# Both units of twelve double groups multiplied in rounded parts, with GpSimd taking the new differences

## Chip, cores and metric

The kernel runs on one core of a Trainium2 chip (trn2). The metric is the time of the program on the device in microseconds, the median of three runs. The core has a matrix engine (PE, with its weight loads shown apart as PEld), VectorE (DVE), ScalarE (ACT), GpSimd (POOL) and SyncE (SP), which here issues nearly all DMAs.

## What is computed

The program is a small vision tower on four images of 512 tokens. Its first step, the embedding, is the part that is changed:

```python
def _L0_tok_ref(xyz, freq_bands, W):          # xyz: [4, 3, 512, 192]
    b, c, n, d = xyz.shape
    xb = 2.0 * jnp.pi * xyz[..., None] * freq_bands          # 6 bands
    feat = jnp.concatenate([jnp.sin(xb), jnp.cos(xb)], axis=-1)
    feat = feat.reshape(b, n, -1)                            # 6912 features
    return jnp.einsum('bnf,of->bno', feat, W)                # W: [192, 6912]

def reference(x, cls_tok, ...):
    h = _L0_tok_ref(x, L0_tok_freq_bands, L0_tok_W)
    h = jnp.concatenate([cls_tok per image, h], axis=1)
    h = h + attention block with relative positions(layernorm(h))
    h = h + second attention and a mixture of 8 experts(layernorm(h))
    return h
```

(Cut; the last lines tell the blocks in words.) For each token the 576 coordinates are multiplied by six frequencies, sine and cosine are taken of each product, and the 6912 features are multiplied by a 192 x 6912 matrix. Everything is float32.

## The kernel before

`program` calls `embed_phase` first, then attention, the second attention and the experts. All phases before and after the embedding are the same in both kernels.

**Groups.** The 576 coordinates of an image lie in five blocks of 128 partitions, for 512 tokens each (tile `x`). A unit is one block and one frequency, 512 columns wide. `GROUPS` lists fifteen groups: twelve double groups with two units (two blocks with one frequency, 1024 columns) and three single ones (the fifth block, 512 columns). `pairs` are the double groups. The four images are passed one after another; for image 0 the weights are loaded and prepared beside the work, the other images find them in SBUF.

**One group.** VectorE computes the product with the frequency, rounded to an integer (`whole`, tile `near`, line 202), subtracts it from the product, which leaves a turn between -0.5 and 0.5 (`reduce`, tile `turn`, line 210), and takes its absolute value (`absolute`, line 216, in the place of `near`). ScalarE takes the sine of the turn (line 347) and the cosine by the sine of the absolute value (line 349), into `feat`. All these tiles are rings of `NF = 3` groups.

**Two kinds of product.** Unit 0 of each group, and single groups, are multiplied natively (`native`, line 417): the float32 features are the stationary operand of PE, the float32 weights `w` with 192 columns the moving one; each float32 product stands in the trace as two records. Four blocks of 128 tokens with sine and cosine make eight products, sixteen records. Unit 1 of each double group is multiplied in rounded parts (`split`, lines 433 to 437): ScalarE casts the features to the rounded type F32R (`first_parts`, line 360), VectorE subtracts that from the features and so has the low part (`rest`, line 227); the weights are taken apart in the same way once, in image 0 (`split_weights`, lines 354 and 221). PE then multiplies high features by high and low weights in one product of 384 columns, and low features by high weights in one of 192, in PSUM banks `sums`, whose columns 0 to 191 and 192 to 383 are added afterwards.

**Order on the engines.** Each engine runs its program in the order of the code. VectorE's `image` does, for group g: `reduce(g)`, `whole(g + 2)`, `absolute(g)`, `rest(g - 1)`; in image 0 `split_weights(g)` follows; in later images `take_sums` of the image before follows in group 1, and `normalize` in group 4. `whole` waits until the cosine three groups back is done, `reduce` until the sine is. ScalarE does sine, cosine and the cast, in image 0 the weights between them, after group 3 the square roots of the image before and after group 10 the transposed tokens. ScalarE's sine waits on `feat_free`, PE's end of the group three back. PE does `native(0)`, `native(1)`, `split`. GpSimd's only work for each image is one addition (line 184, `base`, 128x768) when the sums are taken; SP stores the result with a DMA. `stand_alone` adds one to a semaphore that nobody waits for.

The last image's last three groups are multiplied by `last_groups` in another order, so that the sums end bank by bank.

Of the kernel before, what the change touches and what calls it, by code (L numbers as in the profile page):

```python
# [18 lines left out]
B = 4  # L19
# [50 lines left out]
def embed_phase(nc, s):  # L70
# [9 lines left out]
    w_hi, w_lo, hi_done, lo_done = sem("w_hi"), sem("w_lo"), sem("hi_done"), sem("feat_lo")  # L80
    pairs = [g for g in range(NE) if GROUPS[g][1] == 2]
    NPAIR = len(pairs)
    sums_done, tokens_done, stated, aggregated = sem("sums_done"), sem("tokens_done"), sem("stated"), sem("aggregated")
# [8 lines left out]
    with ExitStack() as ctx:  # L92
        sb = lambda n, sh, dt=F32: ctx.enter_context(nc.sbuf_tensor(n, sh, dt))
        x = sb("x", [128, 5, N])
# [30 lines left out]
        def _(sp):  # L125
            sp.sem_inc(kept, 16)
            sp.dma_start(freq[:, :], s.d["freq_cols"]).then_inc(freq_in, 16)
            for g in range(NE):
# [4 lines left out]
                sp.dma_start(w[:, 2 * g:2 * g + 2, :], s.d["tok_wT"][k0:k0 + 2].rearrange("k p n -> p k n")).then_inc(w_in[g], 16)  # L133
# [38 lines left out]
        def _(pool):  # L172
# [168 lines left out]
        def _(act):  # L341
# [36 lines left out]
            for g in range(NE):  # L378
# [5 lines left out]
                group(0, g, True)  # L384
                if g in pairs:
# [15 lines left out]
        def _(pe):  # L401
            pe.sem_inc(h1_flipped, 2)

            def group(b, g, first):
                n, r = GROUPS[g][1], g % NF
                if first:
                    pe.wait_ge(w_in[g], 16)

                def native(j):
                    pe.wait_ge((sin_done, cos_done)[j], b * NE + g + 1)  # L410
                    k = 2 * g + j
                    for m in range(4):
                        ends = g == NE - 1 and j == 1
                        begins = g == j == 0
                        if begins and not first:
                            pe.wait_ge(tokens_done, b * 4 - 3 + m)
                        mm = pe.matmul(sums[m][:, 0:D], feat[:, r, j, 0, 128 * m:128 * m + 128], w[:, k, :],  # L417
                                       start=begins, stop=ends)
# [4 lines left out]
                def split():  # L423
# [4 lines left out]
                    for j in range(2):  # L428
                        for m in range(4):
                            f = lambda part: parts[:, r, part, j, 128 * m:128 * m + 128]  # L430
                            if g == j == 0:
                                for part in range(2):
                                    pe.matmul(sums[m][:, part * D:part * D + D], f(0), w_parts[:, g, j, part, :], start=False, stop=False)
                            else:
                                pe.matmul(sums[m][:, 0:2 * D], f(0), w_parts[:, g, j, :, :].rearrange("p a n -> p (a n)"),  # L435
                                          start=False, stop=False)
# [2040 lines left out]
```

## Time and profile before

| | us |
|---|---|
| median of three runs (lowest, highest) | 993.34 (992.94, 995.34) |
| the profiled execution, its time | 992.54 |
| its span in the trace | 990.8 |
| PE busy | 896.9 (91%) |
| VectorE busy | 696.6 (70%) |
| ScalarE busy | 645.6 (65%) |
| GpSimd busy | 142.0 (14%) |
| the embedding, from the span's start to the last image's sums | about 290 |

The busy shares are means over stages that differ, so they tell little of one stage; the views by stretch and the timelines do. Times in a timeline row are the start and the duration of one instruction; durations of neighbours on one engine overlap a little, so the distance from start to start tells better what an instruction costs a queue without pauses. Matmul durations overlap by much.

### The profile page before, as it was taken

The numbers are of one execution on the slowest core, as the hardware profiler recorded it, in microseconds if no ns is written. First come the engines' busy times: TensorE is split into PE (matmuls) and PEld (weight loads), VectorE is DVE, ScalarE is ACT, GpSimd is POOL, SyncE is SP. The second block draws the span as 40 slices with busy tenths as digits, with TensorE's granted clock in tenths as the row PEclk, the third lists the DMA queues.
The fourth block names the chain that finished last, engine by engine and source line by source line (L and its number), as shares of the span: only waits on it lengthen the run. The fifth ranks groups of instructions, "written<-read, shape, count | busy, mean of one in ns | idle before, by whom it ended". The sixth has DMA issues, their size and how long they took to land. (4 is left out here: it accounts for less than half of the span.)

```text
span 990.8 us, 19970 instructions
## 1 busy us (share of the span) xinstructions
PE 896.9 (91%) x6459; PEld 794.4 (80%) x6459; DVE 696.6 (70%) x1643; ACT 645.6 (65%) x1218; POOL 142.0 (14%) x204
## 2 busy tenths in 40 slices
PE   6999999999988899989998999898699996699996
PEld 5999999999976677667767776676498875699995
DVE  6889859769633796488648864887556335687775
ACT  5767757649624797589758974987444331886862
POOL 1000000000000144114311441244300000000000
PEclk9999999999997899999999999999789997799997
DMA  8021101089812696169526952795300020443201
GB/s 275 23 71 51 44 27 37 21 125 149 128 34 70 185 293 174 51 210 298 160 58 205 297 156 62 216 294 138 107 1 1 18 87 24 119 164 97 72 2 64
DMA packets 83801, 114.11 MB, mean 115 GB/s; under 512 B 12271, under 2 KB 44476, under 8 KB 83724
## 3 DMA queue, kind: packets, MB, share of 16 engines
q1 hardware_dynamic: 82636, 112.39, 41.2%
q8 instruction: 37, 0.61, 0.3%
q10 hardware_dynamic: 1088, 0.79, 0.2%
q14 instruction: 40, 0.33, 0.1%
HBM read 62.31 MB, written 47.67 MB: 111 GB/s over the span
## 5 line engine op out<-in xcount | busy, mean ns | idle before, releaser
L417 PE MATMUL psum<-w,feat 128*128 128x192 f32 x912 | 160.4, 331 | 11.9 <-ACT feat L347 9.0
L417 PEld LDWEIGHTS psum<-w,feat 128*128 128x128 f32 x912 | 149.3, 192 | 12.8 <-issue 10.3
L646 POOL TENSOR_SCALAR a_scores<-a_scores,a_inv 112x514 f32<-112x514 f32 (+1 forms) x160 | 113.0, 707 | 268.1 <-DVE a_inv L1018 267.9
L1003 DVE CUSTOM_DVE_ANT_0 a_scores<-psum,a_bias 112x514 f32<-112x514 f32 (+1 forms) x160 | 110.0, 688 | 46.6 <-PE psum L722 38.2
L875 ACT ACTIVATE a_scores<-a_scores,a_least 112x514 f32<-112x514 f32 (+1 forms) x160 | 116.7, 729 | 9.8 <-DVE a_least L1003 9.1
L735 PE MATMUL psum<-ident,a_scores 112*112 112x112 f32 (+1 forms) x800 | 100.2, 256 | 18.1 <-DVE a_probsT L1013 10.8
L435 PE MATMUL psum<-w_parts,parts 128*128 128x384 f32 x368 | 113.7, 374 | 0.8 <-DVE parts L227 0.8
L347 ACT ACTIVATE feat<-turn 128x1024 f32<-128x1024 f32 (+1 forms) x60 | 58.4, 974 | 82.5 <-PE psum L437 43.4
L735 PEld LDWEIGHTS psum<-ident,a_scores 112*112 112x112 f32 (+1 forms) x800 | 75.3, 134 | 40.3 <-issue 19.4
L722 PE MATMUL psum<-a_kh,a_q 128*112 128x258 f32 (+1 forms) x320 | 99.6, 333 | 1.0 <-DVE a_least L1003 1.0
L437 PE MATMUL psum<-w_parts,parts 128*128 128x192 f32 x384 | 96.6, 252 | 0.0
L673 PE MATMUL psum<-h1T,place 96*128 (+3 forms) x320 | 87.2, 407 | 4.7 <-DVE a_q L967 2.2
L870 ACT COPY a_probsT<-psum 112x336 f32<-112x336 f32 (+1 forms) x160 | 66.5, 416 | 28.5 <-PE psum L735 24.2
L722 PE MATMUL psum<-a_kl,a_q 128*112 128x258 f32 (+1 forms) x320 | 83.9, 283 | 0.0
L704 PE MATMUL psum<-a_table,a_qpos 96*112 96x257 bf16 (+1 forms) x320 | 66.3, 289 | 10.0 <-ACT a_pos L862 5.4
L862 ACT COPY a_pos<-psum 112x514 f32<-112x514 f32 (+1 forms) x92 | 54.1, 588 | 31.2 <-PE psum L704 28.7
L437 PEld LDWEIGHTS psum<-w_parts,parts 128*128 128x128 f32 x384 | 73.3, 191 | 0.0
L673 PEld LDWEIGHTS psum<-h1T,place 96*128 96x128 f32 (+1 forms) x320 | 59.5, 201 | 15.6 <-DVE a_q L967 2.9
L210 DVE SCALAR_TENSOR_TENSOR turn<-x,freq,near 128x1024 f32<-128x1024 f32 (+1 forms) x60 | 70.9, 1182 | 0.3 <-DVE h1T L331 0.3
L435 PEld LDWEIGHTS psum<-w_parts,parts 128*128 128x128 f32 x368 | 69.2, 188 | 1.3 <-issue 1.3
L202 DVE TENSOR_SCALAR near<-x,freq 128x1024 int32<-128x1024 f32 (+1 forms) x60 | 41.6, 695 | 40.3 <-ACT feat L349 32.5
L349 ACT ACTIVATE feat<-near,half_pi 128x1024 f32<-128x1024 f32 (+1 forms) x60 | 63.3, 1055 | 4.8 <-DVE near L216 4.7
(297 smaller groups left out, 1808.2 us busy)
## 6 DMA issues: line engine op xcount, KB each, us to landing
shear<-a_pos SPq DMA_DIRECT2D x128, 224.9 KB, 3.7
a_bias<-shear SPq DMA_DIRECT2D x128, 224.4 KB, 3.7
shear<-zero SPq DMA_DIRECT2D x20, 448.9 KB, 15.7
e_fc<-in_e_fc_dram SPq DMA_DIRECT2D x16, 384.0 KB, 3.9
x<-in_xT_dram SPq DMA_DIRECT2D x20, 256.0 KB, 3.0
e_proj<-in_e_proj_dram SPq DMA_DIRECT2D x8, 576.0 KB, 5.4
shear<-a_pos SPq DMA_DIRECT2D x32, 130.5 KB
a_bias<-shear SPq DMA_DIRECT2D x32, 130.3 KB
```

Source lines behind the costliest of these rows:

```text
L210: dve.scalar_tensor_tensor(out=turn[:, r, 0:n, :], in0=x[:, c0:c0 + n, :], scalar=freq[:, u:u + 1], in1=near[:, r, 0:n, :], op0=ALU.mult, ...
L417: mm = pe.matmul(sums[m][:, 0:D], feat[:, r, j, 0, 128 * m:128 * m + 128], w[:, k, :], start=begins, stop=ends)
L435: pe.matmul(sums[m][:, 0:2 * D], f(0), w_parts[:, g, j, :, :].rearrange("p a n -> p (a n)"), start=False, stop=False)
L437: mm = pe.matmul(sums[m][:, 0:D], f(1), w_parts[:, g, j, 0, :], start=False, stop=False)
L646: pool.tensor_scalar(row, row, inv[0:TILES[g % NT][1], g % TT:g % TT + 1], 1.0, ALU.mult, ALU.mult).then_inc(weighed, 1)
L673: mm = pe.matmul(out[:, 0:HALF], wt[0:rows, c, 128 * p:128 * p + 128], x, start=c == 0, stop=c == 1)
L704: mm = pe.matmul(pairs[2][w][0:r, 0:HALF], qpos[:, h, i0:i0 + r], table[:, w * HALF:w * HALF + HALF], start=True, stop=True)
L722: mm = pe.matmul(pairs[score_pair(g)][w][0:r, 0:HALF + 1], q[:, h, i0:i0 + r], k[:, h, w * HALF:w * HALF + HALF + 1], start=k is kh, stop= ...
L735: mm = pe.transpose(pairs[3][jb // 3][0:TILE, TILE * (jb % 3):TILE * (jb % 3) + r], scores[0:r, g % TT, TILE * jb:TILE * jb + TILE], s.ide ...
L870: act.copy(probsT[:, slot(g // NT), 0:3, i0:i0 + r], src).then_inc(put_a, 1)
L875: act.activation(scores[0:r, g % TT, 0:PADL], scores[0:r, g % TT, 0:PADL], ACT.Exp, bias=least[0:r, g % TT:g % TT + 1], scale=-1.0, accum_ ...
L1003: dve.tensor_tensor_reduce(halves(scores[0:r, g % TT, 0:PADL]), psum2(score_pair(g), r), halves(bias[0:r, g % MR, :]), -1.0 / 8, BIG, ALU. ...
```

## The change

Unit 0 of every double group now goes the way of unit 1.

- Weights: tile `w` shrinks to the three single groups (`w_native`). The weights of unit 0 of the double groups land in the tile `w_first`, at the place of their low parts; ScalarE casts them into the high parts (`split_first_weights` on ScalarE), GpSimd subtracts in place (`split_first_weights` on GpSimd). This happens in image 0.
- Features: ScalarE casts unit 0 (`high[..., 0, :]`, counted by `first_hi`) and then unit 1, as before. GpSimd subtracts the cast of unit 0 from the features in place (`first_rest`, counted by `first_lo`), VectorE that of unit 1, now in place too. `over` lays a float32 tile and a rounded one over the same memory.
- PE: a double group is `split(1)`, then `split(0)`; each waits for its weights (image 0), its cast and its difference. The first product of an image now is one of 384 columns that starts the accumulation, and it waits for the sums of the image before, bank by bank. Single groups stay as they are.
- GpSimd: the addition for an image comes after `first_rest` of group 3 of the next image.
- The program is built with a smaller scratch for dynamic DMAs (1024).

```diff
         x = sb("x", [128, 5, N])
-        w = sb("w", [128, 2 * NE, D])
+        w_native = sb("w_native", [128, len(native_units), 2, D])
+        w_place, w_first = over("w_first", [128, NFULL, 2, 2, D])
+        first_raw = lambda g: w_place[:, before(g), :, 1, :]
         raw = s.place.rearrange("p (g j n) -> p g j n", g=NPAIR, j=2)
-        feat = sb("feat", [128, NF, 2, 2, N])
+        feat, feat_place = over("feat", [128, NF, 2, 2, N])
         w_parts = sb("w_parts", [128, NPAIR, 2, 2, D], F32R)
-        parts = sb("parts", [128, NF, 2, 2, N], F32R)
+        high = sb("high", [128, NF, 2, 2, N], F32R)
...
-            pool.wait_ge(rows_in, 16)
-            for b in range(B):
+
+            def split_first_weights(g):
+                pool.wait_ge(first_w_hi, before(g) + 1)
+                pool.tensor_tensor(w_first[:, before(g), :, 1, :], first_raw(g), w_first[:, before(g), :, 0, :].bitcast(F32),
+                                   ALU.subtract).then_inc(first_w_lo, 1)
+
+            def first_rest(b, g):
+                r = g % NF
+                pool.wait_ge(first_hi, b * NFULL + before(g) + 1)
+                stand_alone(pool, passed)
+                pool.tensor_tensor(feat_place[:, r, :, 0, :], feat[:, r, :, 0, :], high[:, r, :, 0, :].bitcast(F32), ALU.subtract).then_inc(first_lo, 1)
+
+            def make_base(b):
                 pool.wait_ge(tokens_done, b * 4 + 4)
                 pool.wait_ge(kept, b * 16 + 16)
+                pool.wait_ge(rows_in, 16)
                 pool.tensor_tensor(base[:, :, :], tokens[:, :, :], b2_rows[:, :].unsqueeze(1).broadcast_to([128, 4, D]), ALU.add).then_inc(base_set, 1)
+
+            for g in full:
+                split_first_weights(g)
+                first_rest(0, g)
+            with pool.Fori(1, B) as b:
+                for g in full:
+                    first_rest(b, g)
+                    if g == 3:
+                        make_base(b - 1)
+            make_base(B - 1)
...
-                dve.tensor_tensor(parts[:, r, 1], feat[:, r, :, 1, :], parts[:, r, 0].bitcast(F32), ALU.subtract).then_inc(lo_done, 1)
+                dve.tensor_tensor(feat_place[:, r, :, 1, :], feat[:, r, :, 1, :], high[:, r, :, 1, :].bitcast(F32), ALU.subtract).then_inc(lo_done, 1)
...
+            def split_first_weights(g):
+                act.wait_ge(w_in[g], 16)
+                act.copy(w_first[:, before(g), :, 0, :], first_raw(g)).then_inc(first_w_hi, 1)
+
             def first_parts(b, g):
                 r = g % NF
                 act.wait_ge(sin_done, b * NE + g + 1)
                 act.wait_ge(cos_done, b * NE + g + 1)
-                act.copy(parts[:, r, 0], feat[:, r, :, 1, :]).then_inc(hi_done, 1)
+                if g in full:
+                    act.copy(high[:, r, :, 0, :], feat[:, r, :, 0, :]).then_inc(first_hi, 1)
+                act.copy(high[:, r, :, 1, :], feat[:, r, :, 1, :]).then_inc(hi_done, 1)
...
                 group(0, g, True)
+                if g in full:
+                    split_first_weights(g)
                 if g in pairs:
                     split_weights(g)
                     first_parts(0, g)
...
+                def split(unit):
+                    weights = w_parts[:, g] if unit else w_first[:, before(g)]
                     if first:
-                        pe.wait_ge(w_lo, g + 1)
-                    pe.wait_ge(hi_done, b * NPAIR + g + 1)
-                    pe.wait_ge(lo_done, b * NPAIR + g + 1)
+                        pe.wait_ge(*((w_lo, g + 1) if unit else (first_w_lo, before(g) + 1)))
+                    if unit:
+                        pe.wait_ge(hi_done, b * NPAIR + g + 1)
+                        pe.wait_ge(lo_done, b * NPAIR + g + 1)
+                    else:
+                        pe.wait_ge(first_hi, b * NFULL + before(g) + 1)
+                        pe.wait_ge(first_lo, b * NFULL + before(g) + 1)
                     for j in range(2):
...
+                            if g == j == 0 and unit == 1:
+                                if not first:
+                                    pe.wait_ge(tokens_done, b * 4 - 3 + m)
+                                pe.matmul(sums[m][:, 0:2 * D], hi, both, start=True, stop=False)
                             else:
...
-                mm = native(0)
-                mm = native(1)
-                if n == 2:
-                    mm = split()
+                if g in full:
+                    split(1)
+                    mm = split(0)
+                else:
+                    native(0)
+                    mm = native(1)
...
-    nc = bacc.Bacc("TRN2", target_bir_lowering=False, num_devices=1)
+    nc = bacc.Bacc("TRN2", target_bir_lowering=False, num_devices=1, dynamic_dma_scratch_size=1024)
```

## Rows read from the trace of the kernel before

**Rows 1.** Page, part 1: engine, busy us, share of the span, instructions.

```profile
PE 896.9 (91%) x6459; PEld 794.4 (80%) x6459; DVE 696.6 (70%) x1643; ACT 645.6 (65%) x1218; POOL 142.0 (14%) x204
```

**Rows 2.** Table by stretches: busy us of each engine (instructions), PE clock, DMA.

```profile
160.00:180.00 20.00, 20.00 (x132) 20.00 (x132) 19.75 (x29) 16.96 (x18) 0.00 (x0) 1.00 0.14 46
280.00:300.00 20.00, 16.74 (x99) 15.28 (x100) 10.06 (x29) 4.30 (x8) 2.27 (x6) 0.84 0.05 21
```

**Rows 3.** Timeline of PE, one double group: start, duration, engine, line, tiles, count.

```profile
126.71 2.79 PE L417 MATMUL psum<-w,feat 128*128 128x192 f32 x16
...
129.20 0.47 PE L435 MATMUL psum<-w_parts,parts 128*128 128x384 f32 x1
...
131.59 2.79 PE L417 MATMUL psum<-w,feat 128*128 128x192 f32 x16
```

**Rows 4.** Timeline of VectorE in image 2, one turn of its loop.

```profile
156.32 1.27 DVE L210 SCALAR_TENSOR_TENSOR turn<-x,freq,near 128x1024 f32<-128x1024 f32 x1
157.52 0.74 DVE L202 TENSOR_SCALAR near<-x,freq 128x1024 int32<-128x1024 f32 x1
158.18 0.68 DVE L216 TENSOR_SCALAR near<-turn 128x1024 uint32<-128x1024 uint32 x1
158.78 1.21 DVE L227 TENSOR_TENSOR parts<-feat,parts 128x1024 fp32r<-128x1024 f32 x1
159.92 1.27 DVE L210 SCALAR_TENSOR_TENSOR turn<-x,freq,near 128x1024 f32<-128x1024 f32 x1
```

**Rows 5.** Timeline of ScalarE in image 2, from one sine to the next.

```profile
164.29 1.06 ACT L347 ACTIVATE feat<-turn 128x1024 f32<-128x1024 f32 x1
...
167.59 1.06 ACT L347 ACTIVATE feat<-turn 128x1024 f32<-128x1024 f32 x1
```

**Rows 6.** Timeline of image 0's first group, and the weight split by source line.

```profile
8.97 5.23 PE L417 MATMUL psum<-w,feat 128*128 128x192 f32 x16 [8.97 <-ACT feat L347]
...
9.03 1.15 ACT L349 ACTIVATE feat<-near,half_pi 128x1024 f32<-128x1024 f32 x1 [0.21 <-DVE near L216]
...
10.09 0.49 ACT L354 CAST w_parts<-place 128x384 fp32r<-128x384 f32 x1
...
10.49 1.04 ACT L360 CAST parts<-feat 128x1024 fp32r<-128x1024 f32 x1
...
L221 DVE TENSOR_TENSOR w_parts<-place,w_parts x12: 557/559/559, 10.6 to 64.2; 128x384 fp32r<-128x384 f32 x12
```

**Rows 7.** GpSimd's two-input operations by line: count, ns min/median/max, first and last start.

```profile
L184 POOL TENSOR_TENSOR base<-tokens,b_rows x4: 1803/1810/1813, 82.5 to 289.7; 128x768 f32<-128x768 f32 x4
...
L638 POOL TENSOR_TENSOR a_parts<-a_rest,a_parts x8: 1095/1130/1177, 301.3 to 594.5; 128x514 bf16<-128x514 f32 x8
```

**Rows 8.** Timeline of GpSimd and VectorE where image 1's sums are taken.

```profile
151.10 1.81 POOL L184 TENSOR_TENSOR base<-tokens,b_rows 128x768 f32<-128x768 f32 x1 [66.75 <-DVE tokens L236]
...
152.51 1.48 DVE L210 SCALAR_TENSOR_TENSOR turn<-x,freq,near 128x1024 f32<-128x1024 f32 x1
```

**Rows 9.** A tensor_scalar by source line, and GpSimd's timeline beside its first start.

```profile
L1648 DVE TENSOR_SCALAR t_yn<-y,t_inv x16: 298/308/1878, 706.6 to 737.7; 128x192 f32<-128x192 f32 x16
...
704.69 3.66 POOL L1228 MEMSET t_x<- 1x2048 f32 x2
```

**Rows 10.** Timeline in the attention: a VectorE copy, two GpSimd operations alike.

```profile
580.92 0.67 DVE L939 COPY a_h<-h1T 97x1028 f32 x1
...
579.37 0.70 POOL L646 TENSOR_SCALAR a_scores<-a_scores,a_inv 112x514 f32<-112x514 f32 x1 [0.98 <-DVE a_inv L1018]
...
581.20 0.96 POOL L646 TENSOR_SCALAR a_scores<-a_scores,a_inv 112x514 f32<-112x514 f32 x1 [1.13 <-DVE a_inv L1018]
```

**Rows 11.** Timeline of VectorE after image 1's sums, and line 233 by source line.

```profile
148.83 1.14 DVE L233 COPY tokens<-psum 128x192 f32<-128x192 f32 x4
...
165.12 1.25 DVE L285 TENSOR_SCALAR h_tok<-tokens,mean_var,inv 128x192 f32<-128x192 f32 x4
...
L233 DVE COPY tokens<-psum x12: 343/346/350, 80.2 to 218.5; 128x192 f32<-128x192 f32 x12
```

More of the change, by code:

```diff
@@ L80, in embed_phase @@
     w_hi, w_lo, hi_done, lo_done = sem("w_hi"), sem("w_lo"), sem("hi_done"), sem("feat_lo")
+    first_w_hi, first_w_lo, first_hi, first_lo = sem("first_w_hi"), sem("first_w_lo"), sem("first_hi"), sem("first_lo")
     pairs = [g for g in range(NE) if GROUPS[g][1] == 2]
     NPAIR = len(pairs)
+    full = pairs
+    NFULL = len(full)
+    before = lambda g: sum(e < g for e in full)
+    native_units = [g for g in range(NE) if g not in full]
     sums_done, tokens_done, stated, aggregated = sem("sums_done"), sem("tokens_done"), sem("stated"), sem("aggregated")
@@ L93, in embed_phase, with over @@
         sb = lambda n, sh, dt=F32: ctx.enter_context(nc.sbuf_tensor(n, sh, dt))
+        def over(n, sh):
+            with nc.sbuf_tensor(n, sh, F32) as plain:
+                pass
+            return plain, sb(f"{n}_parts", sh, F32R)
         x = sb("x", [128, 5, N])
-        w = sb("w", [128, 2 * NE, D])
+        w_native = sb("w_native", [128, len(native_units), 2, D])
+        w_place, w_first = over("w_first", [128, NFULL, 2, 2, D])
+        first_raw = lambda g: w_place[:, before(g), :, 1, :]
         raw = s.place.rearrange("p (g j n) -> p g j n", g=NPAIR, j=2)
-        feat = sb("feat", [128, NF, 2, 2, N])
+        feat, feat_place = over("feat", [128, NF, 2, 2, N])
         w_parts = sb("w_parts", [128, NPAIR, 2, 2, D], F32R)
-        parts = sb("parts", [128, NF, 2, 2, N], F32R)
+        high = sb("high", [128, NF, 2, 2, N], F32R)
         near = sb("near", [128, NF, 2, N], I32)
@@ L132, in _ @@
                 k0 = 2 * first_unit[g]
-                sp.dma_start(w[:, 2 * g:2 * g + 2, :], s.d["tok_wT"][k0:k0 + 2].rearrange("k p n -> p k n")).then_inc(w_in[g], 16)
+                first = first_raw(g) if g in full else w_native[:, native_units.index(g)]
+                sp.dma_start(first, s.d["tok_wT"][k0:k0 + 2].rearrange("k p n -> p k n")).then_inc(w_in[g], 16)
                 if g in pairs:
@@ L405, in group @@
                 n, r = GROUPS[g][1], g % NF
-                if first:
+                if first and g not in full:
                     pe.wait_ge(w_in[g], 16)
@@ L410, in native @@
                     pe.wait_ge((sin_done, cos_done)[j], b * NE + g + 1)
-                    k = 2 * g + j
+                    k = native_units.index(g)
                     for m in range(4):
                         ends = g == NE - 1 and j == 1
[L414 to L418, printed above, removed]
+                        mm = pe.matmul(sums[m][:, 0:D], feat[:, r, j, 0, 128 * m:128 * m + 128], w_native[:, k, j, :],
+                                       start=False, stop=ends)
                         if ends:
@@ L428, in split @@
                     for j in range(2):
+                        both = weights[:, j, :, :].rearrange("p a n -> p (a n)")
                         for m in range(4):
[L430 to L433, printed above, removed]
-                            else:
-                                pe.matmul(sums[m][:, 0:2 * D], f(0), w_parts[:, g, j, :, :].rearrange("p a n -> p (a n)"),
-                                          start=False, stop=False)
@@ L437, in split @@
-                            mm = pe.matmul(sums[m][:, 0:D], f(1), w_parts[:, g, j, 0, :], start=False, stop=False)
-                    return mm
-                mm = native(0)
-                mm = native(1)
-                if n == 2:
-                    mm = split()
+                            hi = high[:, r, j, unit, 128 * m:128 * m + 128]
+                            lo = feat_place[:, r, j, unit, 128 * m:128 * m + 128]
+                            if g == j == 0 and unit == 1:
+                                if not first:
+                                    pe.wait_ge(tokens_done, b * 4 - 3 + m)
+                                pe.matmul(sums[m][:, 0:2 * D], hi, both, start=True, stop=False)
+                            else:
+                                pe.matmul(sums[m][:, 0:2 * D], hi, both, start=False, stop=False)
@@ L444, in group @@
+                            mm = pe.matmul(sums[m][:, 0:D], lo, weights[:, j, 0, :], start=False, stop=False)
+                    return mm
+                if g in full:
[4 more added lines that the diff above has]
+                    mm = native(1)
                 if g < NE - 1:
@@ L467, in last_groups @@
                         for j in range(2):
-                            mm = pe.matmul(sums[m][:, 0:D], feat[:, g % NF, j, 0, 128 * m:128 * m + 128], w[:, 2 * g + j, :],
+                            mm = pe.matmul(sums[m][:, 0:D], feat[:, g % NF, j, 0, 128 * m:128 * m + 128], w_native[:, native_units.index(g), j, :],
                                            start=False, stop=g == NE - 1 and j == 1)
```

1 line of the change is left out of this document (removed).

## The prediction

> **What bounds the kernel now.** I read the page's busy table first: the matrix engine (PE) is busy 91% of the span, no other engine over 70% [rows 1]. That mean covers several stages, so I went to the table by stretches. The edit lies in the embedding alone, about the first 290 us, and there PE is busy 20.00 of 20.00 us at full clock, while the stretches behind it, where PE has pauses, come at a lower granted clock [rows 2]. So PE bounds the embedding, and what a double group costs PE is the next view: its timeline shows native matmuls at 126.71, the split ones from 129.20, and the next native ones at 131.59 [rows 3]. A double group is 4.88 us of PE, 2.49 for the native unit and 2.39 for the split one. The other engines follow: VectorE's timeline in a stretch without pauses gives turn 1.20, near 0.66, absolute 0.60, rest 1.14 (start to start), together 3.60 us a group [rows 4]; ScalarE takes 3.30 [rows 5]. Both have over a microsecond of room beside PE's 4.88, and GpSimd is nearly empty. The reader is to see that only PE is full, and then to ask whether the room on the others is really free.
>
> **PE's part.** Unit 0 of each of the 48 double groups (12 in each of 4 images) leaves the native form and takes the form unit 1 has. A split unit runs inside a group at 2.39 less its first, slower pair: 129.20 to 131.59 has eight pairs with about 0.10 of change-over, so 2.29. The group becomes 2 x 2.29 = 4.58 instead of 4.88, a gain of 0.30 us, 48 times, 14 us, if PE stays the bound. The three single groups stay native, 2.49 each.
>
> **ScalarE's part.** One more cast per double group, by the row of the cast that is there (about 1.0 start to start): 3.30 becomes 4.3, still under 4.58. In image 0 one more weight copy of 0.49, started 0.40 before the next instruction [rows 6].
>
> **GpSimd's part, and its price.** The subtraction of 128x1024 is new there. The nearest row is its addition of 128x768 f32 with two inputs from SBUF: 1.81 us; the other two-input form, 128x514 with bf16 output, takes 1.13 [rows 7]. By size these give 2.41 and 2.25. I take 2.35, from the first row, with 0.19 of it as a fixed part (next paragraph). In image 0 come twelve weight subtractions of 128x384, 0.81 + 0.19 = 1.00 by the same row. Rounded output in place is shown by no GpSimd row; VectorE's same step writes rounded output at the plain price, so I add nothing, and allow 2.25 to 2.8. The Trainium skill (GPSIMD Engine Reference, section 3.1) gives 4497 ns for a two-input addition of 2048 columns; half of it is 2.25, an estimate by that page, with which the sum would be about 5 us lower.
>
> **Is VectorE's room free while GpSimd works?** This decides, and the trace has places where both are at work on SBUF. The turn operation, which has two SBUF inputs, takes 1.27 alone [rows 4]; where it starts 0.40 before the end of a GpSimd addition it takes 1.48 [rows 8], longer by 0.20. A tensor_scalar of 0.31 (the median of its line) takes 1.88 when it starts in the middle of a GpSimd memset that ends at 708.35: it was through at 708.47 [rows 9]. So it did not run slower: it stood still until 0.19 before GpSimd's recorded end, and then took its usual time; the turn operation gives the same 0.20. The other way round, GpSimd's 0.70 operation, started in the middle of a VectorE copy between SBUF tiles, took 0.96 [rows 10]. Both wait, and each for the whole of the other's instruction. All four operations of VectorE's embedding loop are of the kinds in these rows: turn and rest have two SBUF inputs, near and absolute are tensor_scalars that read 1024 columns in 0.60 to 0.75, faster than the two-input ones, as the held copy does. So I cost GpSimd's subtraction not beside VectorE's work but in line with it, at 2.35 - 0.19 = 2.16 us.
>
> The Trainium skill (SBUF — State Buffer, section Who interferes with whom) has this as an exclusive lock on a port pair, held for the whole instruction. The rows agree except for the last 0.19 us. By the rule alone the sum would be 48 x 0.19 = 9 us higher; I go by the rows.
>
> **Images 1 to 3.** What must pass one after another is now: twelve groups of 3.60 + 2.16 = 5.76, 69.1 us; three single groups, whose three operations I take at 1.5 (between half and all of the 2.46 of a double group), 4.5; taking the sums, 148.83 to 152.51, 3.7 [rows 8, 11]; normalising, two runs of four at 1.25, 2.5 [rows 11]; GpSimd's own addition, 1.81 - 0.19 = 1.6. One subtraction lies beside the taking of the sums, whose operations read PSUM or one SBUF tile: less 2.2. That is 79.2 us an image against PE's 12 x 4.58 + 3 x 2.49 = 62.4, so VectorE and GpSimd together are the new bound. Before, the additions that follow each image's sums start at 82.5 and, three images on, at 289.7 [rows 7]: 69.1 an image. Longer by 10.1 each, three times 30.
>
> **Image 0.** Here ScalarE's and GpSimd's weight steps stand in the chain too. Count from the end of absolute(g), by the prices above: VectorE does rest(g-1) to 1.1 and then waits for the weight copies; ScalarE does the cosine and two copies, the first ready at 1.6, the second at 2.0; GpSimd splits the first weights from 1.6 and lets go at 2.4; VectorE splits its own (0.5, by its row of 0.56 [rows 6]) to 3.0, then turn(g+1) to 4.2; GpSimd, ready since the cast ended at 2.9, subtracts until 6.3; near(g+3) and absolute(g+1) end at 7.6. So 7.6 us a group. Absolute(0) ends at 9.0, since the cosine starts at 9.03 on its release [rows 6]; absolute(11) then at 92.6. From there the cosine, the copies, the first cast and the subtraction end at 97.8 or so, rest(11) at 99, PE's last double group at 103.6 and three single ones at 111.2. Before, the sums of image 0 are taken from 80.2 on [rows 11]. Longer by 31.
>
> **The sum.** 30 + 31 = 61 us. The profiled execution took 992.5 (span 990.8 and 1.7 around it), the median of the runs is 993.3, 0.8 more. 993.3 + 61 = 1054 us, slower by 6%. What follows the embedding is the same instructions and moves as a block. The kept rows of an image are now added after group 3 of the next; they leave by a DMA that has a whole image of time, so that costs nothing but the 1.6 counted. SP's queue gets no new wait, the weights come in the same number of transfers, and every DMA of the embedding is issued by SP, so the smaller scratch is costed at nothing.
>
> **Clock.** PE would now be busy some 80% in images 1 to 3 and 60% in image 0. In the row of before with 16.74 busy of 20 us the granted clock is 0.84, some of it at the lower level of 1.2 GHz [rows 2]; at that level sixteen native records took 5.23 at the start instead of 2.49 [rows 3, 6]. A double group would then take some 9.2 (twice 4.58), 1.6 over the 7.6 of its turn in image 0. Bounds: nothing, and 12 x 1.6 = 19 us if all of image 0 meets it; images 1 to 3 keep PE fuller. I put nothing into the sum and the 19 into the range.
>
> **Rivals.**
> *The wait is one-sided* (VectorE, once it runs, does not hold GpSimd back, so half an operation, some 0.45 us, is saved at each of 48 subtractions and the weight steps): 1054 - 22 = 1032 us. Against it: 0.96 in place of 0.70 [rows 10].
> *No waiting at all on these operations.* Then PE gains 14; image 0 gives back some 6, since ScalarE's 5.2 a group and the later start of the first product bind there; and each later image gives back about 2: PE used to do the native unit of groups 0 and 1 while VectorE took the sums (3.7) and caught up (3.6 to rest(1)), and now nothing of group 1 can start before rest(1) ends, 7.3 after the sums, while group 0 is through at 1.5 + 4.6 = 6.1; ScalarE's roots cost another microsecond at group 4. 14 - 6 - 6 leaves about 2: 991 us, no difference. For it: the added work fits each engine alone.
> *PE's gain comes through* (the other side): as before, but with the three features in the ring covering those pauses, 14 - 6 = 8 us: 985 us, faster. It decides at the point where VectorE's 3.60 and what GpSimd holds back stay under 4.58, that is if a subtraction costs VectorE less than 1.0 us in place of 2.16. The stretched rows speak against it [rows 8, 9].
>
> **How the numbers follow.** Full waiting both ways 0.80 (1040 to 1085, by three terms: subtraction at 2.25 to 2.8 is 48 x -0.1 to +0.45, -5 to +22; the clock, to +19; and the chain of image 0, in which small waits can fall out, to -10); one-sided 0.08; none 0.05; gain 0.07. The range 1028 to 1085 leaves out the last two and the tails of the first. A measurement here tells about 0.3%, 3 us, from no change: faster 0.07, same 0.05, slower 0.88.
>
> **What would show it.** In the trace of the changed kernel: GpSimd subtractions of 2.2 to 2.8; turn, near, absolute or rest stretched by up to 2.2 in every double group, the sum of VectorE's starts near 5.8 a group; PE idle before its split matmuls, released by VectorE or GpSimd; the additions after the sums some 80 us apart instead of 69; image 0's sums taken near 111. If VectorE's operations keep their lengths, the step on waiting is wrong; if PE's native-free group isn't near 4.6 where nothing waits, the first step is.

## The result, and the profile after

The changed kernel takes 1063.7 us (median of 4 runs, 1057.4 to 1067.4) against 993.1 for the kernel before in the same runs (4 runs, 986.5 to 995.3): a ratio of 1.072, interval 1.067 to 1.077. It is slower by 71 us; the forecast was 1054, slower by 61. The profiled execution took 1064.5, its span 1062.8.

The page of the changed kernel, the span and part 1 (engine, busy us, share of the span, instructions), beside [rows 1]:

```profile
span 1062.8 us, 20166 instructions
...
PE 906.4 (85%) x6443; PEld 797.7 (75%) x6443; DVE 797.9 (75%) x1643; ACT 695.6 (65%) x1278; POOL 307.7 (29%) x264
```

GpSimd has 166 us more, which was meant. VectorE has 101 us more with the same 1643 instructions, which no line of the diff asks for: this is the first thing to see. Where in time, is shown by the changed kernel's table by stretches (busy us of each engine and instructions, then PE clock, DMA share, GB/s); this row stands against the first of [rows 2]:

```profile
160.00:180.00 20.00, 18.02 (x126) 17.31 (x124) 20.00 (x14) 15.01 (x17) 9.92 (x4) 1.00 0.08 27
```

In 160 to 180 PE was busy 20.00 of 20 and VectorE 19.75 with 29 instructions. Now VectorE is busy 20.00 with only 14 and PE 18.02: the full engine has changed. (Nine of the 29 were short operations of the normalising, which fall into another stretch now. The other 20 are the loop's, so the fair comparison is 20 with 14, in which the 20 left room for the nine.) How much the embedding lost is read from the line that takes the sums, which in [rows 11] starts at 80.2 first and 218.5 last. By source line, the changed kernel (count, ns min/median/max, first and last start):

```profile
L270 DVE COPY tokens<-psum x12: 342/342/346, 117.7 to 283.1; 128x192 f32<-128x192 f32 x12
```

The three starts of it are 117.7, 200.0 and 282.3, so an image takes 82.3 where it took 68.6 and 68.9. Image 3's sums are taken bank by bank; its last bank, in VectorE's timeline of the changed kernel and of the kernel before:

```profile
364.43 0.36 DVE L289 COPY tokens<-psum 128x192 f32<-128x192 f32 x1 [0.59 <-PE psum L519]
...
288.91 0.36 DVE L252 COPY tokens<-psum 128x192 f32<-128x192 f32 x1 [0.59 <-PE psum L468]
```

It is ready at 364.4 in place of 288.9. Of these 75.5 us image 0 has 37.5, and the three others 38.0, 12.7 each. Behind the embedding the profiled execution is 3.5 shorter (701.9 to 698.4, spans less embedding). That part lay between 692 and 709 in the profiled executions of this study, so I read nothing into it. 75.5 - 3.5 is the 72.0 between the two profiled executions.

Which instructions of VectorE grew, by line of the changed kernel (tiles, form, count | busy us, mean ns | idle before and what ended it):

```profile
L247 DVE SCALAR_TENSOR_TENSOR turn<-x,freq,near 128x1024 f32<-128x1024 f32 (+1 forms) x60 | 91.2, 1520 | 0.3 <-DVE h1T L368 0.3
L239 DVE TENSOR_SCALAR near<-x,freq 128x1024 int32<-128x1024 f32 (+1 forms) x60 | 79.8, 1332 | 12.9 <-ACT feat L386 8.8 <-DMA x<-in_xT_dram 4.1
L264 DVE TENSOR_TENSOR feat_parts<-feat,high 128x1024 fp32r<-128x1024 f32 x48 | 69.3, 1443 | 4.1 <-ACT high L403 4.1
L253 DVE TENSOR_SCALAR near<-turn 128x1024 uint32<-128x1024 uint32 (+1 forms) x60 | 55.9, 932 | 0.1
```

and the same view of the kernel before:

```profile
L210 DVE SCALAR_TENSOR_TENSOR turn<-x,freq,near 128x1024 f32<-128x1024 f32 (+1 forms) x60 | 70.9, 1182 | 0.3 <-DVE h1T L331 0.3
L227 DVE TENSOR_TENSOR parts<-feat,parts 128x1024 fp32r<-128x1024 f32 x48 | 58.4, 1218 | 0.6 <-ACT parts L360 0.6
L202 DVE TENSOR_SCALAR near<-x,freq 128x1024 int32<-128x1024 f32 (+1 forms) x60 | 41.6, 695 | 40.3 <-ACT feat L349 32.5 <-DMA x<-in_xT_dram 4.2 <-issue 3.6
L216 DVE TENSOR_SCALAR near<-turn 128x1024 uint32<-128x1024 uint32 (+1 forms) x60 | 37.9, 632 | 0.1
```

The instructions are the same in form and number; turn, near, rest and absolute grew from 208.8 to 296.2 us together. A mean hides how; the timeline of VectorE in image 2 of the changed kernel (start, duration) shows it, beside [rows 4]:

```profile
163.81 1.27 DVE L247 SCALAR_TENSOR_TENSOR turn<-x,freq,near 128x1024 f32<-128x1024 f32 x1
165.01 0.74 DVE L239 TENSOR_SCALAR near<-x,freq 128x1024 int32<-128x1024 f32 x1
165.67 2.89 DVE L253 TENSOR_SCALAR near<-turn 128x1024 uint32<-128x1024 uint32 x1
168.48 1.21 DVE L264 TENSOR_TENSOR feat_parts<-feat,high 128x1024 fp32r<-128x1024 f32 x1
169.62 1.27 DVE L247 SCALAR_TENSOR_TENSOR turn<-x,freq,near 128x1024 f32<-128x1024 f32 x1
```

with GpSimd's timeline at that place:

```profile
165.28 2.73 POOL L205 TENSOR_TENSOR feat_parts<-feat,high 128x1024 fp32r<-128x1024 f32 x1 [3.07 <-ACT high L402]
```

In this group three of the four operations have exactly their old lengths. One, absolute, takes 2.89 instead of 0.68. GpSimd's subtraction starts at 165.28 while near is at work (to 165.75) and takes 2.73 instead of its shortest 2.36: it waited for near. Absolute, started at 165.67, then waits for the subtraction, recorded to 168.01. From turn to turn the group is 5.81 us. Which operation is held depends on where the subtraction falls: by the timelines of all four images near is stretched 18 times, turn 10, absolute 9 and rest 7 times, by 88 us together, as much as the four lines grew.

### The profile page after: what moved, and what is told of

It reads as the page before. It is cut to its first block and busy times, and to the rows that moved or that the text cites. A ratio compares the mean times of both kernels' runs of the same rounds, so it can differ in the third digit from the quotient of the medians.

```text
span 1062.8 us, 20166 instructions
## 1 busy us (share of the span) xinstructions
PE 906.4 (85%) x6443; PEld 797.7 (75%) x6443; DVE 797.9 (75%) x1643; ACT 695.6 (65%) x1278; POOL 307.7 (29%) x264
## 5 line engine op out<-in xcount | busy, mean ns | idle before, releaser
L205 POOL TENSOR_TENSOR feat_parts<-feat,high 128x1024 fp32r<-128x1024 f32 x48 | 150.7, 3146 | 135.2 <-ACT high L402 135.2
L485 PE MATMUL psum<-w_parts,high 128*128 128x384 f32 x368 | 125.2, 400 | 50.4 <-DVE feat_parts L264 50.3
L485 PEld LDWEIGHTS psum<-w_parts,high 128*128 128x128 f32 x368 | 77.4, 210 | 56.9 <-issue 56.8
L485 PE MATMUL psum<-w_first_parts,high 128*128 128x384 f32 x384 | 118.8, 373 | 0.0
L486 PE MATMUL psum<-w_parts,feat_parts 128*128 128x192 f32 x384 | 104.5, 272 | 0.0
L486 PE MATMUL psum<-w_first_parts,feat_parts 128*128 128x192 f32 x384 | 98.3, 256 | 0.0
L239 DVE TENSOR_SCALAR near<-x,freq 128x1024 int32<-128x1024 f32 (+1 forms) x60 | 79.8, 1332 | 12.9 <-ACT feat L386 8.8
L486 PEld LDWEIGHTS psum<-w_parts,feat_parts 128*128 128x128 f32 x384 | 83.5, 217 | 0.0
L486 PEld LDWEIGHTS psum<-w_first_parts,feat_parts 128*128 128x128 f32 x384 | 76.6, 200 | 0.0
L485 PEld LDWEIGHTS psum<-w_first_parts,high 128*128 128x128 f32 x384 | 75.9, 198 | 0.0
```

Of the source, the lines that this page charges most:

```text
L205: pool.tensor_tensor(feat_place[:, r, :, 0, :], feat[:, r, :, 0, :], high[:, r, :, 0, :].bitcast(F32), ALU.subtract).then_inc(first_lo, 1)
L239: dve.tensor_scalar(near[:, r, 0:n, :], x[:, c0:c0 + n, :], freq[:, u:u + 1], None, ALU.mult).then_inc(rounded, 1)
L485: pe.matmul(sums[m][:, 0:2 * D], hi, both, start=False, stop=False)
L486: mm = pe.matmul(sums[m][:, 0:D], lo, weights[:, j, 0, :], start=False, stop=False)
```

## The experiments

**The changed kernel without the subtraction.** GpSimd only counts; PE reads the high part in place of unit 0's low part.

```diff
-                stand_alone(pool, passed)
-                pool.tensor_tensor(feat_place[:, r, :, 0, :], feat[:, r, :, 0, :], high[:, r, :, 0, :].bitcast(F32), ALU.subtract).then_inc(first_lo, 1)
+                pool.sem_inc(first_lo, 1)
...
-                            lo = feat_place[:, r, j, unit, 128 * m:128 * m + 128]
+                            lo = feat_place[:, r, j, 1, 128 * m:128 * m + 128] if unit else hi
```

> The changed kernel without GpSimd's subtraction of the features (its semaphore is still counted up); PE takes the high part of unit 0 in place of its low part, so the low part of unit 0 is left out of the sums. GpSimd's weight subtractions in image 0 stay. If VectorE and GpSimd stand in line (theory), an image falls from 82 us to about 68 to 70 and the time to about 1000 us (995 to 1010; image 0 keeps some 10 us for the weights and the later first product). If only the length of the subtraction counts, because PE waits for its result (rival: delay), the same. If the second cast on ScalarE or the new order on PE bounds the embedding (rival: other work), the time stays above 1040.

Measured: 1000.6 us, ratio 1.008 (1.004 to 1.012). 63 of the 71 us go with this one instruction. What is left says that the change would not pay even if GpSimd's work on the features were free (its weight subtractions in image 0 are still there). By source line, and at the last bank of image 3, this kernel without the subtraction:

```profile
L269 DVE COPY tokens<-psum x12: 348/348/351, 92.3 to 230.2; 128x192 f32<-128x192 f32 x12
...
299.06 0.36 DVE L288 COPY tokens<-psum 128x192 f32<-128x192 f32 x1 [0.59 <-PE psum L518]
```

Image 0 has the sums at 92.3, 12 later than before, and the images are 68.2, 68.9 and 69.7 apart, where they were 68.6, 68.9 and 71.2 (the last to image 3's last bank): 2 us less of the 11 that PE's 0.30 would give in 36 groups. The rest goes with waits that PE had less of before. PE's waits in the embedding, this kernel and then the kernel before (line waited for: us in total, times, longest), without those in the first group of image 0:

```profile
PE psum L484 <- DVE feat_parts L263: 15.6, 14, 3.2
PE psum L482 <- DVE tokens L272: 5.1, 3, 1.7
...
PE psum L435 <- DVE parts L227: 0.8, 2, 0.5
...
PE psum L417 <- DVE tokens L236: 2.9, 3, 1.0
```

**The subtraction done, but its result unread.** PE neither waits for it nor reads it; ScalarE waits for it three groups later, before it overwrites the place.

```diff
-                        pe.wait_ge(first_lo, b * NFULL + before(g) + 1)
...
-                            lo = feat_place[:, r, j, unit, 128 * m:128 * m + 128]
+                            lo = feat_place[:, r, j, 1, 128 * m:128 * m + 128] if unit else hi
```

> The changed kernel with GpSimd's subtraction in place, but nobody reads its result: PE takes the high part of unit 0 in its place (the low part is left out of the sums) and does not wait for the subtraction; only ScalarE waits for it, three groups later, before it writes the tile again. Theory, VectorE and GpSimd stand in line: no change against the changed kernel, 1055 to 1070 us, VectorE's operations stretched as there. Rival, delay: about 1000 us, as without the subtraction.

Measured: 1065.7 us, ratio 1.071 (1.059 to 1.083), sums at 116.4, 198.5 and 280.9. PE doesn't wait for the result, GpSimd doesn't appear in ScalarE's waits of this kernel, and the time is that of the changed kernel. So the cost isn't the delay of a late result: it is the presence of the instruction.

**The kernel before, with the same work on GpSimd added.** Once per double group, released by ScalarE's cast as in the change, GpSimd subtracts two private tiles of 128x1024 that nobody reads (the smaller scratch makes room for them).

```diff
+            def unread(b, g):
+                pool.wait_ge(hi_done, b * NPAIR + g + 1)
+                pool.wait_ge(spared, b * NPAIR + g + 1)
+                stand_alone(pool, passed)
+                pool.tensor_tensor(spare[:, :], spare[:, :], turned[:, :], ALU.subtract).then_inc(spared, 1)
```

> The kernel before with one more thing: in every double group GpSimd subtracts two tiles of 128x1024 float32 that nobody else touches, released by ScalarE's cast; nobody waits for it. Theory, standing in line: VectorE's 3.60 us a group and GpSimd's 2.16 come to 5.76 against PE's 4.88; an image grows from 69 to about 79 us, image 0 by about 20, in all 1035 to 1055 us. Rival, delay: 993 us, no change, since nobody waits.

Measured: 1047.8 us (two runs, 1042 and 1053), ratio 1.053 (1.035 to 1.071). The images are 79.8, 79.9 and 79.8 apart, where the forecast's ledger of a later image had 79.2. Neither PE's nor ScalarE's work was touched here. VectorE, by line, in this kernel:

```profile
L231 DVE SCALAR_TENSOR_TENSOR turn<-x,freq,near 128x1024 f32<-128x1024 f32 (+1 forms) x60 | 93.3, 1555 | 0.3 <-DVE h1T L352 0.3
L223 DVE TENSOR_SCALAR near<-x,freq 128x1024 int32<-128x1024 f32 (+1 forms) x60 | 77.4, 1292 | 6.3 <-DMA x<-in_xT_dram 4.4 <-ACT feat L370 1.7
L248 DVE TENSOR_TENSOR parts<-feat,parts 128x1024 fp32r<-128x1024 f32 x48 | 64.7, 1348 | 0.0
L237 DVE TENSOR_SCALAR near<-turn 128x1024 uint32<-128x1024 uint32 (+1 forms) x60 | 64.5, 1075 | 0.1
```

The same four lines grow, by 91 us together against 87 in the change; how the sum is divided among them differs (rest 6 and absolute 27, against 11 and 18). The cost doesn't need the new data flow, the in-place output or the rounded type: GpSimd's subtraction beside VectorE is enough.

**The subtraction done twice.** A second one of the same size follows in the same place (so unit 0's low part is wrong by its high part).

```diff
+                pool.wait_ge(first_once, b * NFULL + before(g) + 1)
+                stand_alone(pool, passed)
+                pool.tensor_tensor(feat_place[:, r, :, 0, :], feat_place[:, r, :, 0, :].bitcast(F32), high[:, r, :, 0, :].bitcast(F32), ALU.subtract).then_inc(first_lo, 1)
```

> The changed kernel with GpSimd's subtraction done twice, the second after the first (so the low part of unit 0 is wrong by the high part). Theory, standing in line: 48 x 2.2 us more, 1064 + 105 = 1170 us (1145 to 1190), a double group near 7.9 us. Rival, delay: GpSimd needs 4.8 us a group, hardly over PE's 4.6 and in parallel with it, so at most some 20 us more, under 1090.

Measured: 1159.5 us (two runs, 1153 and 1166), ratio 1.165 (1.145 to 1.186). The second subtraction costs 1159.5 - 1063.7 = 96 us, 2.0 for each of the 48 (1.9 to 2.1 by the two runs); the first cost 63, 1.3 each. I put the difference down to the room that VectorE had beside PE (4.58 less 3.60 a group): the first subtraction used it up, and the second, with none left, costs nearly the 2.16 that the forecast took for one; no run tests this reading by itself.

**Both differences on VectorE, in one operation of 2048 columns.** GpSimd does nothing for the features.

```diff
+                dve.wait_ge(first_hi, b * NFULL + before(g) + 1)
+                flat = lambda t: t[:, r].rearrange("p j u n -> p (j u n)")
+                dve.tensor_tensor(flat(feat_place), flat(feat), flat(high).bitcast(F32), ALU.subtract).then_inc(lo_done, 1)
```

> The changed kernel with the subtraction of both units on VectorE, as one operation of 128x2048 in place; GpSimd keeps the weight subtractions of image 0 and the additions. Theory: nothing is added but VectorE's 1.07 us a group (1024 columns more at its plain rate), 4.67 against PE's 4.58, and no one holds it up in images 1 to 3; what is lost is at the image's start, where PE waits longer for the first differences: 1005 to 1025 us, clearly under the changed kernel's 1064. Rival, other work (the second cast, PE's order): no better than 1050.

Measured: 1024.7 us, ratio 1.031 (1.022 to 1.040), images 74.1, 73.9 and 72.9 apart. By line, this kernel:

```profile
L263 DVE TENSOR_TENSOR feat_parts<-feat,high 128x2048 fp32r<-128x2048 f32 x48 | 109.7, 2285 | 4.8 <-ACT high L402 4.6
```

The second unit costs VectorE 2.285 - 1.218 = 1.07 us when it does it itself, and 2.2 when GpSimd does it "for" it. Taking the work back to the loaded engine saves 39 us. It still makes VectorE's group 3.60 + 1.07 = 4.67 (4.66 from absolute to absolute in this run, where nothing else comes between), a little over PE's 4.58. That is 1 us for twelve groups; what the images are longer by beyond it is not taken apart here.

**Six groups only, on VectorE.** Unit 0 goes in parts in groups 6 to 11 of images 1 to 3; GpSimd has none of it, and its weights are split in image 0's single groups.

```diff
-    full = pairs
+    full = [g for g in pairs if g >= 6]
...
+                if g in full and not first:
+                    dve.wait_ge(first_hi, b * NFULL - NFULL + before(g) + 1)
+                    flat = lambda t: t[:, r].rearrange("p j u n -> p (j u n)")
+                    dve.tensor_tensor(flat(feat_place), flat(feat), flat(high).bitcast(F32), ALU.subtract).then_inc(lo_done, 1)
+                    return
```

> Unit 0 in rounded parts in groups 6 to 11 of images 1 to 3 alone, its difference in one VectorE operation with that of unit 1; its weights are split while image 0's single groups run, on ScalarE and VectorE. GpSimd does what it does in the kernel before. Theory: away from the image's start VectorE has 4.67 a group against PE's 4.58, so PE's 0.30 us a group comes through, 18 times: 4 to 6 us less than before, 0.995 of it. Rival: VectorE's 4.67 takes it back, no difference.

Measured: 998.1 us (12 runs) against 990.6 (17 runs), ratio 1.006 (1.003 to 1.010): slower, where I expected faster. In its profiled execution, which was also its fastest at 990.7, the embedding does end 1.1 us earlier (287.8 against 288.9). Image 0 loses 3.2 to the weight steps (sums at 83.4) and the later images win back 4.3. That is less than hoped, and what the other runs have on top isn't in that trace. Their times go with their mean granted clock (in the 12 runs some 9 us for each 0.01 of it, in the runs of before 8). This kernel's mean over the runs is 0.960, that of before 0.965; so by that slope more than half of the 6 us between the mean times goes with a lower clock. Why the clock is lower, where, and whether it is the cause of the longer time or goes with the same cause, stays open.

**The smaller scratch alone**, to see whether that was it:

```diff
-    nc = bacc.Bacc("TRN2", target_bir_lowering=False, num_devices=1)
+    nc = bacc.Bacc("TRN2", target_bir_lowering=False, num_devices=1, dynamic_dma_scratch_size=1024)
```

> The kernel before with the smaller scratch for dynamic DMAs and nothing else; every DMA of the program is issued by SP or ScalarE. Theory, the scratch costs nothing, as the prediction has it: ratio 1.000 within 0.3%. Rival: it costs what the version with six groups is slower by than its embedding accounts for, 1.005 to 1.008.

Measured: 992.5 against 993.0, ratio 1.0015 (0.998 to 1.005). It costs nothing that can be measured, as the forecast had it.

**GpSimd that only writes.** The kernel before with a memset of nearly the subtraction's length in its place, 128x2560.

```diff
-                pool.tensor_tensor(spare[:, :], spare[:, :], turned[:, :], ALU.subtract).then_inc(spared, 1)
+                pool.memset(spare[:, :], 1.0).then_inc(spared, 1)
```

> The kernel before plus a GpSimd memset of 128x2560 float32 (some 2.2 us by the rate of 1x2048 in 1.80) in a tile of its own in every double group; it writes and reads nothing. If every VectorE operation of the loop waits for any GpSimd operation, 1035 to 1055 us, as with the subtraction. If those with two SBUF inputs (turn, rest) wait only for one that reads, the memset can lie beside their 2.3 us, and the time stays at 993 to 1010.

Measured: 1010.2 us, ratio 1.016 (1.007 to 1.025), 20 us where the subtraction costs 53 there, and at the upper end of what was expected if turn and rest don't wait. By source line, the kernel with the memset (ns min/median/max):

```profile
L231 DVE SCALAR_TENSOR_TENSOR turn<-x,freq,near x60: 732/1273/1284, 6.7 to 288.6; 128x1024 f32<-128x1024 f32 x48, 128x512 f32<-128x512 f32 x12
...
L248 DVE TENSOR_TENSOR parts<-feat,parts x48: 1205/1213/1226, 15.2 to 286.0; 128x1024 fp32r<-128x1024 f32 x48
...
L223 DVE TENSOR_SCALAR near<-x,freq x60: 471/749/2476, 5.3 to 285.0; 128x1024 int32<-128x1024 f32 x48, 128x512 int32<-128x512 f32 x12
...
L189 POOL MEMSET spare<- x48: 2232/2310/3284, 11.9 to 286.1; 128x2560 f32 x48
```

The median memset is 2.31 long, yet turn and rest, which have two inputs in SBUF, are never longer than 1.284 and 1.226: they don't wait for a GpSimd instruction that only writes. Near, a tensor_scalar, does: up to 2.21 for 0.75 in 1024 columns, and up to 2.48 for 0.47 in 512. The timeline of one group in image 0 has both, a turn beside the memset, with its usual length, and a near held behind it:

```profile
30.01 1.26 DVE L231 SCALAR_TENSOR_TENSOR turn<-x,freq,near 128x1024 f32<-128x1024 f32 x1
30.16 2.23 POOL L189 MEMSET spare<- 128x2560 f32 x1 [3.86 <-ACT parts L381]
31.20 1.75 DVE L223 TENSOR_SCALAR near<-x,freq 128x1024 int32<-128x1024 f32 x1
```

Nearly all of the cost is image 0's (its sums come at 95.0 in place of 80.2). In most groups of the later images near comes first, the memset waits for it and for absolute (3.28 instead of 2.23), and then lies beside rest and turn; these images take about 1 us longer each. The Trainium skill (SBUF — State Buffer, section Who interferes with whom) says both: two-input operations contend with GpSimd's reads and not with its writes, and a tensor_scalar in one of the modes that use two ports contends with GpSimd. The rows agree, as far as near goes by such a mode, which no run here shows by itself.

## Why the prediction was right, and what it missed

**GpSimd and VectorE in line: right, and the cause of the result.** The forecast took 5.76 a group. From absolute to absolute the groups of images 1 to 3 in which nothing else comes between are 5.5 to 5.8 where each has one subtraction (5.81 from turn to turn in the timeline above), and elsewhere come in pairs of 3.6 and 7.9, in which one has none and the next two: 5.75 in the mean. The unread subtraction and the added work on the old kernel show that nothing but GpSimd's subtraction beside VectorE is needed; the second dose has its price. The rival without waiting falls by the unread run (1066 where it would have 991). Its price was 10 us too low besides, as the run without the subtraction shows (1000.6): image 0 gives back 12 instead of 6, and the later images nearly all of PE's gain. For the same reason "PE's gain comes through" (985) had no ground: even without any subtraction only 2 us of it come through.

**Both wait: right.** The one-sided rival (1032) wanted GpSimd to run through. By source line, the changed kernel:

```profile
L205 POOL TENSOR_TENSOR feat_parts<-feat,high x48: 2362/3364/4504, 12.0 to 346.5; 128x1024 fp32r<-128x1024 f32 x48
```

The shortest is 2.36, where I took 2.35 from [rows 7]; the median is 1.0 longer, time in which GpSimd waited for VectorE. So rounded output in place shows no price of its own. Half of the 4497 ns that the Trainium skill gives (GPSIMD Engine Reference, section 3.1), 2.25 as an estimate, is 0.11 under the shortest.

**PE: right.** Where it doesn't wait, a double group is 4.56 (125.41 to 129.97), forecast 4.58. It waits instead: PE's waits in the embedding of the changed kernel, against 0.8 and 2.9 us in the lines of the kernel before that stand with the first experiment:

```profile
PE psum L485 <- DVE feat_parts L264: 50.3, 29, 3.6
...
PE psum L483 <- ACT high L403: 9.5, 3, 3.2
```

**Image 0: the chain right, its end too short.** The groups take 7.4 to 8.4, mostly 7.6 to 7.9, forecast 7.6; absolute(0) ends at 8.9 (9.0) and absolute(11) at 93.9 (92.6). The timeline of one group in the changed kernel shows the chain as it was counted, weights, cast, turn, subtraction, and near held behind the subtraction:

```profile
25.88 1.02 POOL L198 TENSOR_TENSOR w_first_parts<-w_first,w_first_parts 128x384 fp32r<-128x384 f32 x1 [2.82 <-ACT w_first_parts L395]
26.12 1.04 ACT L402 CAST high<-feat 128x1024 fp32r<-128x1024 f32 x1
26.25 1.07 DVE L258 TENSOR_TENSOR w_parts<-place,w_parts 128x384 fp32r<-128x384 f32 x1 [0.90 <-ACT w_parts L391]
...
27.24 1.27 DVE L247 SCALAR_TENSOR_TENSOR turn<-x,freq,near 128x1024 f32<-128x1024 f32 x1
27.34 3.41 POOL L205 TENSOR_TENSOR feat_parts<-feat,high 128x1024 fp32r<-128x1024 f32 x1 [0.44 <-ACT high L402]
28.44 2.87 DVE L239 TENSOR_SCALAR near<-x,freq 128x1024 int32<-128x1024 f32 x1
```

VectorE's weight split (1.07 where it took 0.56) waits for GpSimd's, GpSimd's subtraction (3.41 for 2.36) for turn, and near (2.87 for 0.75) for the subtraction. In two of the twelve groups short operations on the class token come in front of turn; there the subtraction goes first and holds one of these or turn.

The sums are taken at 117.7, not 111.2. Of these 6.5 us 1.3 had come together by absolute(11). Another 1.5 lie up to PE's last double group, because rest(11) stands in VectorE's queue behind three operations of group 12 that I had left out. PE's part is read from its timeline:

```profile
101.84 0.41 PE L485 MATMUL psum<-w_parts,high 128*128 128x384 f32 x1 [1.67 <-DVE feat_parts L264]
...
102.18 0.36 PE L485 MATMUL psum<-w_parts,high 128*128 128x384 f32 x1
...
104.21 0.57 PE L485 MATMUL psum<-w_parts,high 128*128 128x384 f32 x1
...
108.08 7.99 PE L459 MATMUL psum<-w_native,feat 128*128 128x192 f32 x48
...
104.00:106.00 2.00, 2.00 (x9) 2.00 (x9) 1.53 (x6) 0.12 (x1) 0.00 (x0) 0.50 0.43 97
```

The last double group takes 6.24 instead of 4.58, 1.7 more, part of it at the lower level of the clock, 1.2 GHz: the granted clock is 0.50 in the stretch of the last row, and the same 384-column record is 0.57 there and 0.36 in front of it. The single groups take 8.0 in place of 7.6. And the last 1.6 are VectorE, which is in rest(0) of the next image, 2.71 long behind a subtraction, when the sums are ready at 116.1. That clock is what remained of the 19 us in the range: elsewhere in image 0 PE waits anyway.

Two readings under the clock's head in the forecast were not what the rows show. It took the lower level's price from the sixteen native records of 5.23 [rows 6], but the table gives a granted clock of 1.00 for that stretch (9.0 to 14.2), so that row doesn't show it. In the changed kernel at 0.50, a record of 384 and one of 192 columns together go from 0.29 to 0.53 (start to start at 102.18 and at 104.21), so a double group, sixteen such pairs, would by these rows take 8.5 and not 9.2. And of the stretches right behind the embedding those up to 340 us have a lower granted clock (0.82 to 0.84), while those from 340 to 420 have 1.00. Neither reading enters the sum; the first is behind the 19 us of the range.

**Images 1 to 3: the end of the image was mis-sized.** The ledger had 79.2, measured 82.3; this is the term that was too small. From absolute(0) to absolute(11) it holds: eleven groups, the sums, the normalising and GpSimd's addition, 11 x 5.76 + 3.7 + 2.5 + 1.6 - 2.2 = 69.0, measured 68.6. For the single groups and the next group 0 it had 4.5 + 5.76 = 10.3; measured are 2.53, 5.12, 2.01 and 4.09, together 13.8. The timeline of that stretch shows why:

```profile
190.38 7.99 PE L459 MATMUL psum<-w_native,feat 128*128 128x192 f32 x48
190.64 0.63 ACT L384 ACTIVATE feat<-turn 128x512 f32<-128x512 f32 x1 [2.59 <-PE psum L486]
...
192.03 0.75 DVE L239 TENSOR_SCALAR near<-x,freq 128x1024 int32<-128x1024 f32 x1 [1.54 <-ACT feat L386]
...
193.21 1.06 ACT L384 ACTIVATE feat<-turn 128x1024 f32<-128x1024 f32 x1 [1.32 <-PE psum L459]
...
195.46 0.76 DVE L239 TENSOR_SCALAR near<-x,freq 128x1024 int32<-128x1024 f32 x1 [0.87 <-ACT feat L386]
...
201.50 0.44 PE L483 MATMUL psum<-w_parts,high 128*128 128x384 f32 x1 [3.13 <-ACT high L403]
```

PE is late by the waits of the groups before, so ScalarE's sine waits for a place in the ring of three (2.59, 1.32), VectorE waits for ScalarE's cosine (1.54, then 0.87, and 0.26 at 188.2), and PE then waits 3.13 for group 0. In VectorE's three waits, 2.7 us together, GpSimd has nothing to do either. They are nearly all of the 3.0 that an image is longer than the ledger. (The two parts above are cut at absolute; rest runs a group behind, so 1.1 of the 13.8 belong to the eleven groups, and the 0.87 lies in them.) The ledger counted only what these two must do one after another; it took them as never idle. Three images at 3.0 are 9.1 us, less 1.4 because the images of before took 69.6 in the mean and not 69.1; with 6.5 of image 0 and 3.5 off behind the embedding that is 10.7, the distance from the 61.3 forecast (30.3 and 31) to the 72.0 of the profiled executions.

## What to carry to other kernels

Before moving work to GpSimd, look at what kinds of operation VectorE runs beside it: if they read two inputs from SBUF, or are tensor_scalars and copies of the kinds above, and GpSimd's instruction reads SBUF too, add GpSimd's duration to VectorE's loop as if VectorE did it, and compare that sum with the bound, not each engine's own share. If GpSimd only writes, only the tensor_scalars and GpSimd hold each other (1.6% here, against 5.3%). In this kernel doing the extra work on VectorE itself (1.07 us) was cheaper than having it taken off (2.2 us), and where the Trainium skill (Perfetto Trace Analysis, section Optimizing Scalar/DVE Operations) says that offloading between these two "might not help", the measurement here is a loss: 1063.7 us with GpSimd doing it, 1024.7 with VectorE. To tell such a cost from a late result, run the operation with its result unread.

## What was not expected of the hardware

A GpSimd memset holds VectorE's tensor_scalars (a near of 512 columns took 2.48 for 0.47) but leaves two-input operations of VectorE alone (1.28 and 1.23 at most), so whether GpSimd's instruction reads decides whom it holds. A run's time goes with its mean granted clock by some 8 us for each 0.01, which goes with most of the spread of 985 to 999 among runs of the kernel before; an edit of a few microseconds can be lost in that, and in the version with six groups the clock's mean over the runs was itself lower by 0.004, for a reason that these runs don't show.
